# Merging an attention head by four transposes and a sum over groups, in place of four matmuls with a selection matrix

## The reference

```python
q = _qdq(x) @ _qdq(wq).T + bq
kv = cond @ wkv.T + bkv
k, v = jnp.split(kv, 2, axis=-1)
attn = jax.nn.softmax(jnp.einsum('bnhd,bmhd->bhnm', q, k) * scale, axis=-1)
o = jnp.einsum('bhnm,bmhd->bnhd', attn, v).reshape(B, N, C)
out = _qdq(o) @ _qdq(wp).T + bp
```

## Time and profile before

| | us |
|---|---|
| median of 3 runs | 634.84 (630.89 to 636.75) |
| the profiled execution | 635.79 |
| its span | 634.0 |
| busy: TensorE matmuls | 611.2 (96%) |
| busy: VectorE | 369.5 (58%) |
| busy: ScalarE | 299.6 (47%) |
| busy: GpSimd | 228.5 (36%) |

### The profile page before, as it was taken

How to read it: one execution, slowest core, us unless ns; L and a number is a source line. 1 busy time by engine, 2 the same in 40 slices (tenths; PEclk the granted TensorE clock), 3 DMA queues, 4 the chain that set the end, 5 groups by cost and what they waited for, 6 DMA issues and landing times.

```text
span 634.0 us, 12622 instructions
## 1 busy us (share of the span) xinstructions
PE 611.2 (96%) x4456; PEld 488.9 (77%) x4456; DVE 369.5 (58%) x680; ACT 299.6 (47%) x424; POOL 228.5 (36%) x120
## 2 busy tenths in 40 slices
PE   8999999999999999999999999999897999989998
PEld 7877788888887667777677777666797988789996
DVE  3996530330436778887787778855654234366652
ACT  4444233233233555555555555564257557544441
POOL 2000200000011878788888887770003533410000
PEclk9999999999999999999999999999998978999999
DMA  8873644524548666655566666600130334145520
GB/s 306 291 236 121 193 156 154 199 90 165 173 143 260 155 158 162 160 145 145 149 162 156 161 152 165 158 1 3 67 132 8 127 103 162 68 146 191 195 66 33
DMA packets 29758, 92.19 MB, mean 145 GB/s; under 512 B 5472, under 2 KB 9568, under 8 KB 23008
## 3 DMA queue, kind: packets, MB, share of 16 engines
q1 hardware_dynamic: 28480, 89.67, 46.9%
q10 hardware_dynamic: 1248, 2.10, 0.9%
HBM read 65.02 MB, written 18.35 MB: 131 GB/s over the span
## 4 chain that ended last, share of the span: by engine, by line
PE 87%; DVE 4%; ACT 3%; issue 2%; POOL 2%; DMA 1%; POOLq 0%; SPq 0%; ACTq 0%; DVEq 0%
PE ps L340 17%; PE ps L341 16%; PE ps L342 16%; PE ps L1293 10%; PE ps L1390 9%; PE ps L1402 9%; PE ps L1416 4%; POOL p_sum L581 1%; PE ps L1376 1%; PE ps L1378 1%; DMA k_stack<-kh_scratch 1%; PE ps L1222 1%; PE ps L1589 1%; PE ps L1576 1%; ACT probs L751 1%
## 5 line engine op out<-in xcount | busy, mean ns | idle before, releaser
L700 ACT ACTIVATE p_ring<-ps 128x1024 f32<-128x1024 f32 x128 | 125.7, 1022 | 101.6 <-PE ps L1390 74.4
L962 DVE TENSOR_REDUCE m_part<-ps 128x1 f32<-128x512 f32 x240 | 150.4, 684 | 29.1 <-PE ps L1293 26.2
L581 POOL TENSOR_TENSOR p_sum<-p_sum,p_ring 128x1024 f32<-128x1024 f32 x60 | 142.8, 2381 | 9.0 <-ACT p_ring L700 4.7
L1293 PE MATMUL ps<-k_stack,q_max 96*128 96x512 f32 x240 | 86.9, 422 | 1.1 <-DMA k_stack<-kh_scratch 0.6
L1390 PE MATMUL ps<-q_stack,k_stack 98*128 98x256 f32 x512 | 80.7, 286 | 0.2 <-ACT p_ring L700 0.2
L1390 PEld LDWEIGHTS ps<-q_stack,k_stack 98*128 98x128 f32 x512 | 74.7, 189 | 7.8 <-ACT p_ring L700 1.4
L1402 PE MATMUL ps<-p_ring,v_head 128*32 128x256 f32 x1024 | 71.6, 383 | 0.1
L340 PE MATMUL ps<-xt_h,h_ring 128*128 128x256 f32 x208 | 58.9, 283 | 1.2 <-DVE xt_l L1076 1.2
L1293 PEld LDWEIGHTS ps<-k_stack,q_max 96*128 96x128 f32 x240 | 40.8, 188 | 23.8 <-DVE m_part L962 13.4
L341 PE MATMUL ps<-xt_l,h_ring 128*128 128x256 f32 x208 | 58.5, 281 | 0.0
L342 PE MATMUL ps<-xt_h,l_ring 128*128 128x256 f32 x208 | 58.4, 281 | 0.0
(11 more groups left out here) (188 smaller groups left out, 1065.8 us busy)
## 6 DMA issues: line engine op xcount, KB each, us to landing
f_ring<-stream SPq DMA_DIRECT2D x29, 1024.0 KB, 4.9
k_stack<-kh_scratch SPq DMA_DIRECT2D x60, 256.0 KB, 4.6
kh_scratch<-kh_buf SPq DMA_DIRECT2D x32, 256.0 KB, 5.4
kl_scratch<-kl_buf SPq DMA_DIRECT2D x32, 256.0 KB, 6.0
v_head<-v_all SPq DMA_DIRECT2D x16, 512.0 KB, 3.0
k_stack<-kl_scratch SPq DMA_DIRECT2D x30, 256.0 KB, 4.2
v_all<-stream SPq DMA_DIRECT2D x4, 256.0 KB, 4.7
f_ring<-stream SPq DMA_DIRECT2D x4, 256.0 KB, 5.5
```

Source lines behind the costliest of these rows:

```text
L581: nc.gpsimd.tensor_tensor(p_sum[:, p, :], p_ring[:, 0, :] if n == 0 else p_sum[:, p, :], p_ring[:, c % 4, :], ALU.add).then_inc(sums_done, 1)
L700: nc.scalar.activation(p_ring[:, c % 4, :], ps[:, 2 * (c % 2):2 * (c % 2) + 2, :].rearrange("p b n -> p (b n)"), ACT.Exp, scale=XSCALE).th ...
L962: nc.vector.reduce_max(m_part[:, j // NT, j % NT:j % NT + 1], maximum_bank(j), AX.X).then_inc(max_read, 1)
L1293: nc.tensor.matmul(maximum_bank(j), q_max[p][0:SPLIT_ROWS, at128(j % NT)], k_stack[p][0:SPLIT_ROWS, j // NT * D:(j // NT + 1) * D], start= ...
```

## The change

`merge` no longer multiplies with `pick`. TensorE transposes the four 128 x 128 blocks of `o_t` (two of outputs, two of denominators) with the fp32 identity, and all 512 columns of bank 4 are written: tokens on partitions, and in each block of 128 columns the four groups of 32 side by side. VectorE adds the groups: one `tensor_reduce` gives `den` (two blocks, one column of each group, 8 values a partition), a second gives `o_sum` (two blocks, 32 sums of four values that stand 32 columns apart, 256 values a partition). Reciprocal and scaled addition follow, now from SBUF. The matrix `pick` and the nine GpSimd instructions that made it are gone. Each step waits for the one before through a counter, which is why 8 steps for two heads become 12.

```diff
-        pick = sb("pick", [P, DH + 1], F32)
...
+        den = sb("den", [P, NT], F32)
+        o_sum = sb("o_sum", [P, NT, DH], F32)
...
-            for tile in (ident, ident_b, pick):
+            for tile in (ident, ident_b):
                 order.step(nc.gpsimd.memset(tile[:], 0.0))
...
-            for first in range(0, P, DH):
-                order.step(nc.gpsimd.affine_select(out=pick[:, 0:DH], in_=pick[:, 0:DH], compare_op=ALU.not_equal,
-                                                   fill=1.0, base=-first, pattern=[[-1, DH]], channel_multiplier=1))
...
             def normalize_output(h):
                 dve.wait_ge(merge_done, h + 1)
-                order.step(nc.vector.reciprocal(r_den[:], bank(4).rearrange("p (t c) -> p t c", c=64)[:, 0:NT, DH]))
+                groups = bank(4).rearrange("p (u g d) -> p u d g", u=2 * NT, d=DH)
+                order.step(nc.vector.tensor_reduce(den[:], groups[:, NT:2 * NT, 0, :], axis=AX.X, op=ALU.add))
+                order.step(nc.vector.tensor_reduce(o_sum[:], groups[:, 0:NT, :, :], axis=AX.X, op=ALU.add))
+                order.step(nc.vector.reciprocal(r_den[:], den[:]))
                 for t in range(NT):
-                    nc.vector.scalar_tensor_tensor(out=o_all[:, t, bass.ts(h, DH)], in0=bank(4)[:, 64 * t:64 * t + DH],
+                    nc.vector.scalar_tensor_tensor(out=o_all[:, t, bass.ts(h, DH)], in0=o_sum[:, t, :],
                                                    scalar=r_den[:, t:t + 1], in1=bv_row[:, bass.ts(h, DH)],
                                                    op0=ALU.mult, op1=ALU.add).then_inc(o_done, 1)
...
-                order.enter(4, i, 8)
+                order.enter(4, i, 12)
...
-                for t in range(NT):
-                    nc.tensor.matmul(bank(4)[:, 64 * t:64 * t + DH], o_t[:, at128(t)], pick[:, 0:DH],
-                                     start=True, stop=True)
-                    last = nc.tensor.matmul(bank(4)[:, 64 * t + DH:64 * t + DH + 1], o_t[:, at128(NT + t)],
-                                            pick[:, DH:DH + 1], start=True, stop=True)
+                for t in range(2 * NT):
+                    last = nc.tensor.transpose(bank(4)[:, at128(t)], o_t[:, at128(t)], ident[:])
                 last.then_inc(merge_done, 1)
```

More of the change, by code:

```diff
@@ L555, in _ @@
                                         pattern=[[-1, P]], channel_multiplier=1).then_inc(consts_ready, 1)
-            for first in range(0, P, DH):
-                order.step(nc.gpsimd.affine_select(out=pick[:, 0:DH], in_=pick[:, 0:DH], compare_op=ALU.not_equal,
-                                                   fill=1.0, base=-first, pattern=[[-1, DH]], channel_multiplier=1))
-                order.step(nc.gpsimd.affine_select(out=pick[:, DH:DH + 1], in_=pick[:, DH:DH + 1],
-                                                   compare_op=ALU.not_equal, fill=1.0, base=-first,
-                                                   pattern=[[-1, 1]], channel_multiplier=1))
             nc.gpsimd.memset(ones_col[:], 1.0).then_inc(ones_set, 1)
```

## The result

The changed kernel takes 641.72 us (median of 4 runs, 640.53 to 642.62), the kernel before 632.87 us (4 runs, 629.88 to 636.75). The ratio is 1.0138, with a 95% interval of 1.009 to 1.0186: slower by 8.8 us, where the forecast was 635.6 us, within 1% of before, and a range that ended at 640.5 us.

A forecast was written before the change was run, and what follows sets the result against it. The prediction took TensorE's wait for fetched keys in 13 heads as the bound. Its terms, 0 + 0.3 + 0.3 + 0.2 = +0.8 us, on a 634.84 us median gave 635.6 us, range 631.0 to 640.5 us.

The forecast's parts named there:

- the wait for the keys: In 13 heads, TensorE at the first maximum (j = 0) waits for fetched keys; claimed to be the wait ending last.
- part 2: VectorE's merge chain: two more reductions in series, 0.65 us longer, net 0.61 us; loop cost +0.3 us.
- TensorE saves 0.47 us per merge: TensorE's merge: weight loads span 0.43 us instead of 0.90 us; the saving counts 0 in the 13 heads with a fetch.
- Rival A: TensorE's saving in the heads comes through: 631.0 us with ScalarE's cap of 0.33 us, 629.2 us without; chance 0.10.
- The reductions: 0.20 and 0.45 us: VectorE's added merge reductions: 0.20 us for the denominators, 0.45 us for the sum of outputs, assuming the stride costs nothing.
- Rival B: VectorE becomes the bound if strided short groups read slower: 638.8 us at a 0.68 us reduction; chance 0.12.
- j = 1 needs 0.78 us and finds 0.70 to 0.90 us: In the loop, maximum j = 1 waits for scaled outputs; five of 13 distances fall short, together +0.3 us.
- Last head +0.3, final merge +0.2 us: Last two merges: TensorE ends 0.35 and 0.42 us earlier, VectorE's chain is 0.65 us longer: +0.3 and +0.2 us.
- rival C: TensorE's clock falls in the heads' stretch: its 192.3 us grow by 23.8 us, to about 658 us; chance 0.03.

The follow-up runs named there:

- the half merge: The kernel before, without the two matmuls of each merge that sum the denominators (four of eight on TensorE): 631.55 us, ratio 0.9995.
- the early keys: The kernel before, with the first half of each head's keys fetched as two quarters, the first already after score chunk 1: 630.69 us, ratio 0.9944.
- the old merge with the SBUF input: The kernel before, but VectorE copies the 64 summed outputs from PSUM to SBUF and the scaled additions read that copy: 649.38 us, ratio 1.0273.

## Why the prediction was wrong

The reading of the kernel was right in its main point, that TensorE's saving is lost in the wait for the keys. One sentence of part 2 was wrong, and it alone carried the time out of the range. Point by point:

- *TensorE saves 0.47 us per merge and it is worth 0 in 13 heads.* The 0 is right: the half merge shows it (0.9995), and the early keys show why (14.89 to 14.63 us). The 0.47 us is too much. From the first load to those of the next chunk it is 0.52 us, not 0.43 us, since the next chunk's load follows the fourth after 0.18 us and not after 0.11 us; by the matmuls' starts 0.40 us are saved. ScalarE would have capped the saving at 0.18 us anyway. Rival A put that at 0.33 us, from the last of the 13 heads, where score chunk 7 starts 0.38 us after the exponential; in the other twelve it is 0.33 us, and the slower restart was left out.
- *The reductions: 0.20 and 0.45 us.* Right: 0.19 us from start to start for the denominators, 0.46 us for the outputs, of which 0.42 us are the instruction itself. The stride of 32 values costs nothing here. Rival B with its price for short groups did not happen, though its mechanism, VectorE's chain in front of j = 1, is the one that decided.
- ***"The reciprocal and the two scaled additions stay as they are (the latter now read SBUF: no change counted)."*** **This is the step that failed.** The first takes 1.01 us instead of 0.25 us. I had costed an edit of an operand at nothing, without naming a row for it, and without bounding it, although no row of the trace had two SBUF inputs beside a GpSimd instruction that reads SBUF; the one beside a memset gave no warning.
- *j = 1 needs 0.78 us and finds 0.70 to 0.90 us.* The way of reckoning held, though not term by term: j = 1 starts 0.055 us after the outputs and not 0.17 us, but what follows it comes 0.42 to 0.44 us behind it instead of 0.32 to 0.33 us, which makes up for the difference. With 0.76 us more it needs 1.54 us: twelve distances, which sum to 9.5 us, miss it by 12 x 1.54 - 9.5 = 9.0 us, and the first by 0.15 us. That is 9.1 us, and 9.0 us are what stands between the starts of the merges in head 14 (417.36 and 426.37 us).
- *Last head +0.3, final merge +0.2 us.* Nearly right: 0.20 us more between the last two merges, 0.26 us more from the last merge to the first step behind it (1.99 to 2.25 us). GpSimd is silent there.
- *The clock falls in the heads (rival C).* Not in the changed kernel, with four transposes and up to 1.15 us from j = 0 to j = 1 in each head: 1.00. It did in the old merge with the SBUF input, in four heads.

With the sum in PSUM, the kernel that the prediction in fact described, the ratio is 1.0033, which is 2.1 us with an interval from 0.1 to 4.0 us; +0.8 us was predicted. The profiled executions have 0.5 us up to the last merge and 0.3 us from there to the first step behind it (1.99 to 2.27 us).

The Trainium skill's rule on the shared ports (SBUF — State Buffer, Who interferes with whom) would have given the right answer from rows of before, this one among them:

```profile
314.04 2.38 POOL L581 TENSOR_TENSOR p_sum<-p_sum,p_ring 128x1024 f32<-128x1024 f32 x1 [0.40 <-ACT p_ring L700]
```

GpSimd's addition starts 0.17 us after the maximum j = 14 begins to be read (313.87 us) and reads two SBUF tiles. It is still under way when the scaled additions are due 0.61 us later than before, at 315.46 us, and would hold them until 316.4 us.

## What to carry to other kernels

When an edit moves an operand of a VectorE instruction from PSUM to SBUF, look at what GpSimd does at that moment: the instruction may have to wait for the end of GpSimd's current one, and a result that is read once and soon is better left in PSUM. A share of the critical chain is no promise: ask which wait ends last behind the place that gets faster, and test it by taking work away there alone before building the faster version. And an operand that changes its memory is a part of the change with a price of its own, to be bounded like any other.

## What the runs showed of the hardware

- A scaled addition of 32 columns, 0.25 us by itself, lasted, beside GpSimd's addition, until 0.05 us after the end of that addition, in 14 heads of the changed kernel and in 14 of the old merge with the copy, however early it had begun (it took 0.94 to 1.15 us and 1.28 to 1.44 us). A multiplication of one SBUF tile of 32 columns did the same (0.94 to 1.14 us, 0.24 us by itself). With one input in PSUM the scaled addition took 0.25 us beside the same GpSimd addition.
- A subtraction of two SBUF tiles beside a GpSimd memset, and a `tensor_scalar` of one column beside GpSimd's addition, took no longer than by themselves (2.28 us, 0.20 to 0.22 us).
- A reduction of 64 x 4 values at a stride of 32 columns from PSUM takes 0.42 us, on the line of the contiguous ones, and 0.43 us if it writes PSUM.
- Four fp32 transposes of 128 x 128 take 0.60 us from the first start to the last end, and four matmuls of the same weights with 32 columns 0.53 us; for both it is 0.52 us from the first weight load to the next score chunk's. That the four weight loads set the pace of both is a reading of this, not tested by itself.
- Behind a wait TensorE also restarts more slowly: j = 1's matmul starts 0.055 us after the outputs that it waited for, but the matmuls behind it come 0.42 to 0.44 us after it instead of 0.32 to 0.33 us.
- A fetch that ends last also passes its scatter on: with it the heads took 14.73 to 14.96 us, without it 14.61 to 14.63 us.
